# An LSTM stage regrouped: gates G and I each in a bank and with a tanh of their own, G sharing its bank with O

## The reference

```python
def step(carry, xt):
    h, c = carry
    z = xt @ w_ih.T + b_ih + h @ w_hh.T + b_hh
    i, f, g, o = jnp.split(z, 4, axis=-1)
    c = jax.nn.sigmoid(f) * c + jax.nn.sigmoid(i) * jnp.tanh(g)
    h = jax.nn.sigmoid(o) * jnp.tanh(c)
    return ((h, c), h)
...
agg = jnp.matmul(A_norm, x)
out = jax.nn.sigmoid(jnp.matmul(agg, lw))
```

## Time and profile before

| what | us |
|---|---|
| median of 3 runs | 1655.46 |
| lowest and highest run | 1655.4 and 1659.48 |
| span of the profiled execution, first to last instruction | 1639.5 |
| recurrent stage, first to last product of the cell | 1276.8 to 1586.6 |
| output stage | from about 1587 to the end |

### The profile page before, as it was taken

How to read it: one execution, slowest core, us unless ns; L and a number is a source line. 1 busy time by engine, 2 the same in 40 slices (tenths; PEclk the granted TensorE clock), 3 DMA queues, 4 the chain that set the end, 5 groups by cost and what they waited for, 6 DMA issues and landing times. The chain is left out here.

```text
span 1639.5 us, 29449 instructions
## 1 busy us (share of the span) xinstructions
PE 1193.5 (73%) x6017; PEld 791.5 (48%) x6048; DVE 1204.1 (73%) x4351; ACT 753.6 (46%) x2049; POOL 708.6 (43%) x1122
## 2 busy tenths in 40 slices
PE   4777777887788777778346656566656988888884
PEld 2444444444444444444235545454545655655564
DVE  3899999999999999997368888888884333333337
ACT  2656665666566656665122222232321333333347
POOL 4454545555555555555255656565663000000006
PEclk9999999999999999998667787877787999999989
DMA  4666667565666565665000000000100000000003
GB/s 96 145 168 140 163 139 169 135 164 139 161 147 165 140 171 138 169 135 143 16 20 14 26 13 26 13 26 13 33 10 5 1 0 0 0 0 0 0 1 104
DMA packets 128148, 128.86 MB, mean 79 GB/s; under 512 B 60867, under 2 KB 107359, under 8 KB 128097
## 3 DMA queue, kind: packets, MB, share of 16 engines
q1 hardware_dynamic: 126372, 127.19, 31.3%
q10 hardware_dynamic: 1725, 1.13, 0.2%
HBM read 123.05 MB, written 5.21 MB: 78 GB/s over the span
## 5 line engine op out<-in xcount | busy, mean ns | idle before, releaser
L738 PE MATMUL wf<-hid,w2t 128*128 128x384 f32 x512 | 206.6, 528 | 47.9 <-DVE msg L911 47.5
L545 POOL TENSOR_TENSOR sum<-msg 128x384 f32<-128x384 f32 (+1 forms) x128 | 143.0, 1117 | 67.6 <-DVE msg L911 67.1
L738 PEld LDWEIGHTS wf<-hid,w2t 128*128 128x128 f32 x512 | 89.7, 195 | 124.4 <-issue 92.0
L1642 POOL MEMSET r_minus_half<- 128x4 f32 x1 | 0.1, 101 | 328.3 <-POOLq L1512 328.3
L1590 DVE SCALAR_TENSOR_TENSOR r_new<-r_gates 128x64 f32<-128x64 f32 x128 | 28.8, 225 | 148.1 <-ACT r_gates L1571 148.1
L528 POOL TENSOR_TENSOR rf_r<-rf,rf_hi 128x128 f32<-128x128 f32 x64 | 27.7, 433 | 253.5 <-ACT rf_hi L668 253.5
L911 DVE SCALAR_TENSOR_TENSOR msg<-wf,b2c,rv 128x768 f32<-128x768 f32 x128 | 129.2, 1010 | 6.7 <-PE wf L738 5.9
L884 DVE TENSOR_TENSOR rv<-rg,sq_bc 128x768 f32<-128x768 f32 x128 | 121.2, 947 | 10.7 <-DMA sq_bc<-edge_sq 6.2
L723 PE MATMUL zb<-gauss,w1t 64*128 64x384 f32 x256 | 117.8, 541 | 14.2 <-ACT expd L643 10.8
L643 ACT ACTIVATE expd<-zb,safe_b,reached 128x768 f32<-128x768 f32 x128 | 124.7, 974 | 0.7 <-PE zb L724 0.7
L724 PE MATMUL zb<-gauss,w1t 64*128 64x384 f32 x256 | 118.6, 544 | 0.0
(11 more groups left out here) (273 smaller groups left out, 3562.0 us busy)
## 6 DMA issues: line engine op xcount, KB each, us to landing
sq_bc<-edge_sq SPq DMA_DIRECT2D x64, 768.0 KB, 7.1
val_bc<-edge_val SPq DMA_DIRECT2D x128, 192.0 KB, 4.9
idx_bc<-edge_idx SPq DMA_DIRECT2D x64, 384.0 KB, 5.4
adj_w<-in_adj_rows SPq DMA_DIRECT2D x64, 64.0 KB, 4.5
xt_w<-in_x_cols SPq DMA_DIRECT2D x64, 64.0 KB, 4.9
xin<-in_x_rows SPq DMA_DIRECT2D x32, 128.0 KB, 5.2
m_adj_g<-in_adj_rows SPq DMA_DIRECT2D x16, 256.0 KB, 2.6
m_adjt_g<-in_adj_t SPq DMA_DIRECT2D x16, 256.0 KB, 2.6
```

What stands on the lines that cost most here:

```text
L545: pool.tensor_tensor(sum1[:, 0:wide, :], m[:, 0:wide, :], m[:, wide:2 * wide, :], ALU.add)\
L738: last = pe.matmul(wf[:, half, 0:HALF], w2t[:, :], hid[:, q, half * HALF:(half + 1) * HALF], start=True, stop=True)
```

## The change

Gates G and I no longer share a bank. I has the bank `z_i` to itself, G lies in the first quarter and O in the second quarter of `z_go`, F stays in `z_f`. The bias matmuls of G, I and F now have the start flag, and O's has none. Each gate's recurrent matmul has an increment of its own, so there is a `zg_ready` and a `zi_ready` in place of `zgi_ready`. ScalarE does G's tanh and I's tanh one after the other, 64 columns each, with `g_ready` and `i_ready`. TensorE waits for `g_ready` ahead of O's recurrent matmul, because ScalarE reads the bank that this matmul writes. VectorE's `new` waits for `g_ready` and then for `i_ready`. The output stage uses `z_go` where it used `z_o`. The diff, whole:

```diff
@@ -1489,25 +1489,24 @@
         gates = sb("gates", [P, 4, B])
         cell = sb("cell", [P, B])
         keep, new, tanh_c = sb("keep", [P, B]), sb("new", [P, B]), sb("tanh_c", [P, B])
-        (start_ready, zgi_ready, zf_ready, zo_ready, gi_ready, f_ready, new_ready, keep_ready, cell_ready, tanh_ready,
-         h_ready) = (sem(n) for n in ("start_ready", "zgi_ready", "zf_ready", "zo_ready", "gi_ready", "f_ready",
+        (start_ready, zg_ready, zi_ready, zf_ready, zo_ready, g_ready, i_ready, f_ready, new_ready, keep_ready, cell_ready,
+         tanh_ready, h_ready) = (sem(n) for n in ("start_ready", "zg_ready", "zi_ready", "zf_ready", "zo_ready", "g_ready", "i_ready", "f_ready",
                                       "new_ready", "keep_ready", "cell_ready", "tanh_ready", "h_ready"))
 
 
-        z_gi = [c0.enter_context(nc.psum_tensor(f"r_zgi{i}", [P, 2, 4, B], F32)) for i in range(2)]
+        z_i = [c0.enter_context(nc.psum_tensor(f"r_zi{i}", [P, 2, 4, B], F32)) for i in range(2)]
         z_f = [c0.enter_context(nc.psum_tensor(f"r_zf{i}", [P, 2, 4, B], F32)) for i in range(2)]
-        z_o = [c0.enter_context(nc.psum_tensor(f"r_zo{i}", [P, 4, 2 * B], F32)) for i in range(2)]
+        z_go = [c0.enter_context(nc.psum_tensor(f"r_zgo{i}", [P, 4, 2 * B], F32)) for i in range(2)]
         I_, F_, G_, O_ = range(4)
 
         def z_of(bank, q):
 
-            if q == G_:
-                return z_gi[bank][:, 0, :, :]
             if q == I_:
-                return z_gi[bank][:, 1, :, :]
+                return z_i[bank][:, 0, :, :]
             if q == F_:
                 return z_f[bank][:, 0, :, :]
-            return z_o[bank][:, 0:2, :].rearrange("p a (t b) -> p (a t) b", b=B)
+            part = z_go[bank][:, 0:2, :] if q == G_ else z_go[bank][:, 2:4, :]
+            return part.rearrange("p a (t b) -> p (a t) b", b=B)
 
         with ExitStack() as c1:
             block = c1.enter_context(nc.Block())
@@ -1527,18 +1526,18 @@
                 def inputs(t, bank, q):
 
                     z = z_of(bank, q)
-                    pe.matmul(z, bias_parts[:, q, :], ones[:, :], start=q in (G_, F_, O_), stop=False,
+                    pe.matmul(z, bias_parts[:, q, :], ones[:, :], start=q in (G_, I_, F_), stop=False,
                               skip_group_check=True)
                     pe.matmul(z, w_ih[:, q, :], dyn[:, bass.ds(t, 4), :], start=False, stop=False,
                               skip_group_check=True)
 
-                def recurrence(bank, j, h):
-
-                    for q, ready in ((G_, None), (I_, zgi_ready), (F_, zf_ready), (O_, zo_ready)):
-                        last = pe.matmul(z_of(bank, q)[:, j, :], w_hh[:, q, :], h, start=False, stop=True,
-                                         skip_group_check=True)
-                        if ready is not None:
-                            last.then_inc(ready, 1)
+                def recurrence(bank, j, h, n):
+
+                    for q, ready in ((G_, zg_ready), (I_, zi_ready), (F_, zf_ready), (O_, zo_ready)):
+                        if q == O_:
+                            pe.wait_ge(g_ready, n)
+                        pe.matmul(z_of(bank, q)[:, j, :], w_hh[:, q, :], h, start=False, stop=True,
+                                  skip_group_check=True).then_inc(ready, 1)
 
                 order = (G_, I_, F_, O_)
 
@@ -1554,7 +1553,7 @@
                         else:
                             pe.wait_ge(h_ready, t + j)
                             h = hs[:, bass.ds(t + (j - 1), 1), :]
-                        recurrence(bank, j, h)
+                        recurrence(bank, j, h, t + (j + 1))
                         if not final:
                             inputs(t + 4, 1 - bank, order[j])
                         pe.matmul(idle_p[:, :], idle[:, 0:P], idle[:, :], start=True, stop=True)
@@ -1565,10 +1564,12 @@
                 def body(t, bank, first, final):
                     for j in range(4):
                         n = t + (j + 1)
-                        act.wait_ge(zgi_ready, n)
+                        act.wait_ge(zg_ready, n)
                         if not (first and j == 0):
                             act.wait_ge(h_ready, t + j)
-                        act.activation(gates[:, 0:2, :], z_gi[bank][:, :, j, :], ACT.Tanh).then_inc(gi_ready, 1)
+                        act.activation(gates[:, 0, :], z_of(bank, G_)[:, j, :], ACT.Tanh).then_inc(g_ready, 1)
+                        act.wait_ge(zi_ready, n)
+                        act.activation(gates[:, 1, :], z_of(bank, I_)[:, j, :], ACT.Tanh).then_inc(i_ready, 1)
                         act.wait_ge(zf_ready, n)
                         act.activation(gates[:, 2, :], z_of(bank, F_)[:, j, :], ACT.Tanh).then_inc(f_ready, 1)
                         act.wait_ge(zo_ready, n)
@@ -1586,7 +1587,8 @@
                 def body(t, bank, first, final):
                     for j in range(4):
                         n = t + (j + 1)
-                        dve.wait_ge(gi_ready, n)
+                        dve.wait_ge(g_ready, n)
+                        dve.wait_ge(i_ready, n)
                         dve.scalar_tensor_tensor(new[:, :], gates[:, 1, :], 1.0, gates[:, 0, :], ALU.add, ALU.mult)\
                             .then_inc(new_ready, 1)
                         dve.wait_ge(f_ready, n)
@@ -1612,7 +1614,7 @@
                  "offset_ready y_dve y_act consts").split()
         s = {n: sem(n) for n in names}
         stored = [sem(f"stored{i}") for i in range(4)]
-        lwt_b = [z_o[i][:, :, :] for i in range(2)]
+        lwt_b = [z_go[i][:, :, :] for i in range(2)]
         o_b = [idle_p[:, :].rearrange("p (a n) -> p a n", a=G),
                c0.enter_context(nc.psum_tensor("r_o1", [P, G, P], F32))[:, :, :]]
         NGR = B // G
```

## The result

The changed kernel is 7% slower: 1772.82 us by the median of four runs (1767.78 to 1775.85), against 1657.47 for the kernel before (1655.40 to 1695.69). The ratio is 1.070, with a 95% interval from 1.067 to 1.073. The forecast was 1655.5 us with a range from 1651 to 1661.

What follows compares the result with a forecast made beforehand. The prediction took the recurrent stage to be bound by a chain of latencies, 128 steps of 2.44 us. Every part of the change was valued at 0, so 0 x 128 = 0 left 1655.5 us, range 1651 to 1661.

Steps and rivals of the forecast that it cites:

- The chain: Recurrent step: G, I and F's passes, F's tanh, keep, cell, tanh_c, h; a step stays at 2.44 us.
- The part on new: VectorE's new, behind a separate wait for I's tanh, starts at 1.10; value 0, ends 0 and 5.1 us.
- The clock falls: Slower rival: TensorE's clock drops in the recurrent stage, 0.48 us more a step, eleven steps 5.3 us; chance 0.02.
- O's wait reaches the chain: Slower rival: TensorE's stop ahead of O's passes delays tanh_c or the next step; 12.8 us, 1668; chance 0.03.
- F's tanh was held by the joint tanh: Faster rival: on ScalarE F's tanh could start at 0.94 of a step; 7.7 us gained, 1647.8; chance 0.08.
- TensorE's 77 us are mostly the matmuls for the next four steps and the idle one: Recurrent stage: TensorE's busy 77 of 90 us are mostly input and idle matmuls, cover and not the bound.
- The increments serialize: Slower rival: TensorE's signals delay F's end by 0.03 us a step; 3.8 us, 1659.3; chance 0.03.

Runs made afterwards that it cites:

- e5: The changed kernel, but VectorE's new waits for I's tanh alone, without the wait for G's; 1636.8 us beside 1636.3, ratio 1.000.
- e8: The changed kernel with a second idle matmul, of 256 columns, in each step; 1638.2 us beside 1636.3, ratio 1.001.
- e1: The changed kernel with the next group's bias matmul moved ahead of TensorE's wait before O's product; 1751.5 us, ratio 1.058.
- e3: The kernel before with G's and I's tanh as two activations, new waiting for both, banks and TensorE's list unchanged; 1781.1 us, ratio 1.075.
- e6: The kernel before with a second, long met wait (for I's matmul) ahead of VectorE's new; ratio 1.000.
- e9: The changed kernel with new's two waits swapped, I's tanh first and G's second; 1652.1 us beside 1658.1, ratio 0.997.
- e11: The kernel before with an idle matmul of 448 columns in place of 512; 1751.7 us, ratio 1.056.
- e4: The kernel before with an idle matmul of 384 columns in place of 512; 1765.2 us, ratio 1.067.
- e14: The kernel before with two VectorE operations of 8 columns between new and keep in one step of eight, keep 0.127 us late there; ratio 1.057.
- e17: The kernel before with one VectorE operation of 48 columns between new and keep in one step of eight, keep 0.091 us late there; ratio 1.035.
- e18: e14 with a second idle matmul of 256 columns in each step; 1657.1 us beside 1655.6, ratio 1.002.
- e16: e5 with two VectorE operations of 32 columns between new and keep in one step of eight; runs of 1744.14, 1746.73, 1720.71 and 1657.22 us.
- e13: The kernel before with one VectorE operation of 8 columns between new and keep in one step of eight, keep 0.050 us late there; ratio 1.001.
- e15: e5 with two VectorE operations of 8 columns between new and keep in one step of eight, keep 0.075 us late there; ratio 1.001.

## Why the prediction was wrong

- *The chain, and each of its terms in a plain step.* Right, to 0.02 us in the starts, as the step above shows, and e5 shows it in time: with the late step gone the same layout, tanhs, increment and stop give a ratio of 1.000.
- *The part on new.* Right in the middle, wrong at the edge. The separate wait was foreseen, with new at 1.10, no room left, and up to 0.04 us a step if it went badly (128 x 0.04 = 5.1 us). What came was 0 in seven steps of eight and 0.09 in the eighth (0.35 in the first turn), 1.5 us in all by e8. I had read one step and taken it for 128. The trace of the kernel before already showed that steps are not alike: 2.26 us where they are written out, 2.41 to 2.49 in the loop, and fourteen branches of the loop behind the last product of a turn (line 1519). Why the separate instruction makes just that step late is not settled: the separate wait itself starts in time there (1324.6, as I's tanh ends), and new starts 0.4 behind it, where 0.07 is usual. (The row at 1064.43, from which the 1.10 was taken down, has one separate wait ahead of it in the trace, not two.) It happens with a late wait (the changed kernel, e1, e3, e8) and hardly with an early one (e6, e9).
- *The clock falls*, the rival at 0.02, is what happened, and this is the step of the prediction that failed: "The passes per step stay and only 0.06 of TensorE's pause moves". The price I gave it, 0.48 us a step for eleven steps, was too low in both factors: 1.05 us for 108 steps. I took the step of the stage's end, where the input matmuls are missing; with them TensorE's list at 1.2 GHz is longer than the chain. The kernel before has only two of those steps, and nothing stood behind the number eleven. And I had asked how much the change moves, but not how close the kernel stood to the fall. The idle matmul at line 1560, whose result nobody reads, was the sign that someone had to hold the clock up, and its length the thing to doubt. e11 measures the distance: less than 64 of its 512 columns. The kernel before seems to fall over by itself now and then: five of its 82 runs took 1690 to 1696 us, and the four of them with a clock on record have a mean of 0.87 to 0.88, against 0.90 to 0.92 for the others. None of the five was profiled, so that it is this stage is not shown.
- *O's wait reaches the chain*: it didn't. O's load moved by 0.07 us (0.06 was worked out), and e5, with the same stop, has the time of the kernel before.
- *F's tanh was held by the joint tanh*: refuted. F's tanh stays 0.22 behind I's in the changed kernel, though ScalarE can take them 0.11 apart (e3).
- *TensorE's 77 us are mostly the matmuls for the next four steps and the idle one*: that was too strong. By line, the recurrent passes are busy 40.0 us of the 90, the bias, input and idle matmuls 46.6 (they overlap, so the sum is above 77). The forecast did not rest on it.
- *The increments serialize*: no sign. G's last pass signals, and I's and F's passes follow as before. The estimate from the Trainium skill ("TensorE: Matmul & The Clock Gate", The cost: per-tile semaphore tail), whose figure is for tiles packed side by side in the array, was 3.3 us; it is not seen in e5, whose interval ends at 1.001, 1.6 us.
- What stays open: by what rule the chip decides. In the runs less work in a step (e4, e11), longer steps (e3) and late steps once in eight (e14, e17) each lose it, and more idle work keeps it (e8, e18). Open too is why the changed kernel falls sooner (44 us) than e1 (102 us), which has the same late steps but no stop ahead of O, and sooner than e17 (259 us), which lacks the 0.35 us step as well. The stop and that step may have a share, but neither was added to the late steps of e17, and e1's longest run was as long as the changed kernel's. Chance has a part: e16 lost the clock in three runs of four.

## What to carry to other kernels

Where an idle matmul holds the clock, first measure how much of it can be taken away before the clock falls; if it is a little, no small change to the chain can be judged by its own latency, and more idle columns can buy room: with 256 more a step, late steps that had lost the clock no longer did, at ratios of 1.001 and 1.002 (e8, e18). When an instruction waits for two things, write the late one first, or leave out the wait that the other implies: of two waits the second was a separate instruction of the sequencer, in either order (line 1591, above and in e9). And walk through all steps of a loop's turn; here the last one was the late one.

## What the runs showed of the hardware

- Once lost, the clock isn't regained in the stage in any trace here, though TensorE then shows busy 355 of 360 us. In the kernel before TensorE is busy only 77 of 90 us in the earlier trace rows and keeps it.
- The level changes the bound: at 2.4 GHz the step is the chain's 2.45 us; at 1.2 GHz TensorE's list makes it 3.50, 3.39 with 384 idle columns and 3.11 with none.
- On VectorE an instruction whose second wait is separate, and the late one, starts 0.10 us after the releaser's end, against 0.03 otherwise; ScalarE takes tanhs of 64 columns from PSUM 0.11 us apart.
- In the kernel before, one step in eight late by 0.09 us is enough to lose the clock (e17, in all five runs); by 0.05 it is not (e13, ten runs), nor by 0.075 in the layout of e5 (e15, ten runs).
